# Two attentions over a short context and a self-attention on one core: one list of blocks for all three

## What is computed

```
x  = attention16(x Wq, c Wk, c Wv) + x                     # "a0": 16 heads of 16, 77 keys
n  = layernorm(x);  x = x + Wo attention16(n, n, n)        # "a1": self-attention, 1024 keys
n  = layernorm(x);  x = x + Wco attention16(n, c, c)       # "a2": 77 keys
n  = layernorm(x);  x = x + W2 gelu(W1 n + b1) + b2        # 256 -> 1024 -> 256
```

## Time and profile before

| | |
|---|---|
| median of 3 executions | 869.67 us (863.86, 869.67, 871.61) |
| profiled execution | 873.17 us, its span 871.4 us |
| mean granted TensorE clock | 0.926 of full speed |
| busy: PE, DVE, ACT, POOL | 753.0, 523.6, 424.8, 119.3 us |
| HBM read, written | 36.33 MB, 28.22 MB |

### The profile page before, as it was taken

The page is one execution under the profiler, slowest core; times in us unless marked ns, Lnnn a source line. Parts: engine busy times, 40 slices in busy tenths (PEclk is TensorE's granted clock), DMA queues, the critical chain, the costliest instruction groups (busy, mean ns, idle before and its releaser), DMA issues.

```text
span 871.4 us, 12781 instructions
## 1 busy us (share of the span) xinstructions
PE 753.0 (86%) x4848; PEld 375.3 (43%) x4848; DVE 523.6 (60%) x805; ACT 424.8 (49%) x770; POOL 119.3 (14%) x241
## 2 busy tenths in 40 slices
PE   6428768749899999999999999998978788999998
PEld 3225433334443333333343433333444354457767
DVE  1225465268879999999979998851364456240001
ACT  2105423402068888888767767664534334422120
POOL 9601014021000000000001101020031002130000
PEclk9758878978899999999999999996899899999999
DMA  7765540562580404040404010124154530000001
GB/s 247 209 208 128 111 116 25 185 156 100 197 167 2 76 2 76 3 76 2 75 3 74 3 24 11 44 94 77 41 138 108 137 57 4 1 0 25 19 15 40
DMA packets 37565, 66.95 MB, mean 77 GB/s; under 512 B 6848, under 2 KB 17216, under 8 KB 37504
## 3 DMA queue, kind: packets, MB, share of 16 engines
q1 hardware_dynamic: 37216, 66.05, 30.0%
q10 hardware_dynamic: 288, 0.08, 0.0%
HBM read 36.33 MB, written 28.22 MB: 74 GB/s over the span
## 4 chain that ended last, share of the span: by engine, by line
PE 56%; DVE 21%; SPq 8%; DMA 7%; ACT 3%; issue 3%; POOL 2%; DVEq 0%; POOLq 0%; ACTq 0%
PE PV L727 13%; DVE nm L918 13%; PE ST L711 11%; PE ST L619 5%; PE ST L615 5%; PE SM L656 4%; SPq L476 4%; DMA stacks<-mrow 3%; PE SM L606 3%; PE SM L596 3%; PE SM L600 2%; PE SM L663 2%; POOL stacks L1014 2%; SPq L533 2%; PE PV L619 2%
## 5 line engine op out<-in xcount | busy, mean ns | idle before, releaser
L816 ACT ACTIVATE prob<-ST 128x512 f32<-128x512 f32 (+1 forms) x640 | 344.6, 595 | 215.1 <-PE ST L711 207.0
L918 DVE TENSOR_REDUCE nm<-SM 128x2 f32<-128x1024 f32 x256 | 308.8, 1221 | 18.6 <-PE SM L656 17.0
L727 PE MATMUL PV<-prob,Vst 128*32 128x256 f32 (+1 forms) x2304 | 208.1, 434 | 7.3 <-ACT pvT L805 6.7
L711 PE MATMUL ST<-stacks 64*128 64x512 f32 x512 | 133.9, 506 | 1.5 <-DVE split L852 1.3
L656 PE MATMUL SM<-stacks 64*128 64x512 f32 x512 | 111.3, 430 | 21.2 <-DMA stacks<-k_rows 11.7
L711 PEld LDWEIGHTS ST<-stacks 64*128 64x128 f32 x512 | 51.1, 186 | 111.0 <-ACT prob L816 91.2
L727 PEld LDWEIGHTS PV<-prob,Vst 128*32 128x32 f32 x2304 | 46.6, 110 | 103.6 <-issue 77.4
L921 DVE TENSOR_REDUCE nm<-SM 128x8 f32<-128x624 f32 x64 | 51.5, 805 | 64.1 <-PE SM L663 62.8
L711 PE MATMUL ST<-stacks,Kc 128*77 128x512 f32 x128 | 52.4, 491 | 34.2 <-DMA stacks<-mrow 32.8
L656 PEld LDWEIGHTS SM<-stacks 64*128 64x128 f32 x512 | 49.9, 189 | 44.2 <-DVE nm L918 22.9
L1084 POOL CAST mp<-na 128x16 fp32r<-128x16 f32 x48 | 9.6, 199 | 417.0 <-DVE na L953 253.5
(11 more groups left out here) (98 smaller groups left out, 674.5 us busy)
## 6 DMA issues: line engine op xcount, KB each, us to landing
q_rows<-split SPq DMA_DIRECT2D x72, 256.0 KB
stacks<-q_rows SPq DMA_DIRECT2D x48, 384.0 KB
k_rows<-split SPq DMA_DIRECT2D x24, 256.0 KB
stacks<-k_rows SPq DMA_DIRECT2D x16, 384.0 KB
stacks<-mrow SPq DMA_DIRECT2D x192, 4.0 KB
fm<-in_xT SPq DMA_DIRECT2D x4, 512.0 KB, 8.8
X<-in_x SPq DMA_DIRECT2D x4, 512.0 KB, 4.5
V<-in_w SPq DMA_DIRECT2D x2, 1024.0 KB, 9.5
```

Source lines behind the costliest of these rows:

```text
L711: mm(ST[0:att.keys, n % 3, :], keys_of(att, g, h, kt), QST[att.name][g % att.buffers][rows, h // 2, j * BLK:(j + 1) * BLK], start=True, st ...
L727: last = mm(PV[h * 32:(h + 1) * 32, queries], Vst[:, g % 2, kt, h, :], prob[:, t % 2, h, queries], start=(kt == 0 and first == 0), stop=(k ...
L816: act_fn(prob[0:att.keys, t % 2, h, :], ST[0:att.keys, n % 3, :], ACT.Exp, scale=SCALE) \
L918: ins = vec.tensor_reduce(nm[:, q % 2, c, tile, 2 * n:2 * n + 2], ps.rearrange("p (s k) -> p s k", s=2), AX.X, ALU.max, negate=True)
```

## The change

Blocks of all three attentions now stand in one list, cut into three parts: `FIRST_PART` (a0), `LONG_PART` (a1's 16 blocks, and among the last four of them a2's eight blocks of batch 0, in pairs), `LAST_PART` (a2's eight blocks of batch 1). The blocks are numbered through; maxima, rows, outputs and semaphores count by that number. With it:

- Batch 1's residual adds, norms, transposes, eight chunks and eight value projections move from the list ahead of a1 to steps 1 to 41 of `LONG_PART`. The self-attention output projection and a2's queries of batch 0 stand at steps 67 to 90, one item a step instead of one in two.
- Batch 0's feed-forward (`up` 0 and 1, `down` 0 and 1) moves into `BEFORE_LAST`, ahead of batch 1's a2; `AFTER_LAST` keeps batch 1's.
- a0 and a2 get query buffers of their own, `Qx`, three instead of four, and values of their own, `Vx`. a1 has two stack buffers instead of three, `split` three instead of four. The query projection of a2 and the output projection keep weights of their own.
- Stacks are issued at steps set by hand: a0's group g at step 2g - 4, a1's at 16g - 16, a2's group 7 at step 2 of `LAST_PART`.
- a1's lead is 24 units instead of 26.
- The first memsets (keys' stack, three query stacks, zeros) move from POOL to DVE, ahead of DVE's copy of the context. The DMA that clears the rows of maxima reads 128 columns sixteen times instead of 1024 columns twice. The order of the chunks under a0's last steps is by features first; a1's first stack is issued at step 14 of a0.

```diff
-SB = 4
+SB = 3
...
-A0 = Attention(0, 1, CTX, lead=6, rows_ahead=2, rows_at=0, buffers=4, under=UNDER_A0)
-A1 = Attention(1, SEQ // P, P, lead=26, rows_ahead=1, rows_at=4, buffers=3, under=UNDER_A1)
-A2 = Attention(2, 1, CTX, lead=6, rows_ahead=2, rows_at=0, buffers=4, under=UNDER_A2)
+A0 = Attention(0, 1, CTX, buffers=3)
+A1 = Attention(1, SEQ // P, P, buffers=2)
+A2 = Attention(2, 1, CTX, buffers=3)
...
+class Part:
+
+    def __init__(self, blocks, lead):
+        self.b0, self.t0, self.lead = len(BLOCKS), len(STEPS), lead
+        for att, q in blocks:
+            BLOCK_AT[att.name, q] = len(BLOCKS)
+            FIRST.append(len(STEPS))
+            STEPS.extend((len(BLOCKS), kt) for kt in range(att.kt))
+            BLOCKS.append((att, q))
+        self.steps = len(STEPS) - self.t0
+        self.last = self.steps + 3
+        self.under = {}
+        stream = [("max", b, v) for b in range(self.b0, len(BLOCKS)) for v in range(BLOCKS[b][0].units)]
+        ends, n = {}, 0
+        for b in range(self.b0, len(BLOCKS)):
+            n += BLOCKS[b][0].units
+            ends[b] = n
+        self.before = list(stream[:lead])
+        pending = list(range(self.b0, len(BLOCKS)))
+        added = 0
+        while pending and ends[pending[0]] <= lead - 1:
+            b = pending.pop(0)
+            late = 4 if BLOCKS[b][0].whole else 1
+            self.before.insert(min(ends[b] + late, lead) + added, ("rows", b, 0))
+            added += 1
+        self.work, done = [], lead
+        for i in range(self.last):
+            upto = min(len(stream), lead + 2 * (i + 1))
+            work = [((k + 1) * QUAD // (upto - done) - 1, w) for k, w in enumerate(stream[done:upto])]
+            if pending and ends[pending[0]] <= done:
+                work.append((2, ("rows", pending.pop(0), 0)))
+            done = upto
+            if 2 <= i < self.steps + 2:
+                b, kt = STEPS[self.t0 + i - 2]
+                if kt == BLOCKS[b][0].kt - 1:
+                    work.append((3, ("out", b, 0)))
+            self.work.append(work)
...
+FIRST_PART = Part([(A0, q) for q in range(NQ)], lead=6)
+LONG_PART = Part([(A1, q) for q in range(13)] + [(A2, 0), (A2, 1), (A1, 13), (A2, 2), (A2, 3), (A1, 14), (A2, 4), (A2, 5),
+                                                 (A1, 15), (A2, 6), (A2, 7)], lead=24)
+LAST_PART = Part([(A2, q) for q in range(NQ // 2, NQ)], lead=6)
+for tb in range(NB):
+    FIRST_PART.put(tb, ("load", tb))
+for g in range(3, NG):
+    FIRST_PART.put(2 * g - 4, ("stack", "a0", g))
+FIRST_PART.put(8, ("load", 4), ("load", 5))
+FIRST_PART.put(9, ("x1", 0))
+FIRST_PART.put(10, ("norm", 0, 0), ("x1", 1), ("load", 6), ("load", 7))
+FIRST_PART.put(11, ("norm", 0, 1), *block_of("t_ln1", 0))
+FIRST_PART.put(12, ("proj_q1", 0, 0), ("proj_k1", 0, 0), *block_of("t_ln1", 1))
+FIRST_PART.put(13, ("proj_q1", 1, 0), ("proj_k1", 1, 0))
+FIRST_PART.put(14, ("proj_q1", 0, 1), ("proj_k1", 0, 1), ("stack", "a1", 0))
+FIRST_PART.put(15, ("proj_q1", 1, 1), ("proj_k1", 1, 1))
+LONG = LONG_PART.at
+LONG_PART.put(1, ("x1", 2), ("keys", "a2"))
+LONG_PART.put(4, ("x1", 3))
+LONG_PART.put(5, ("norm", 0, 2))
+LONG_PART.put(7, *block_of("t_ln1", 2))
+LONG_PART.put(8, ("norm", 0, 3))
+LONG_PART.put(10, *block_of("t_ln1", 3))
+LONG_PART.row(11, 2, halves(("proj_q1", "proj_k1"), (2, 3)) + block_of("vals_s", 2) + block_of("vals_s", 3))
+LONG_PART.row(LONG(A1, 8, 3), 1,
+              block_of("t_a1", 0) + block_of("out_1", 0) + [("stats", 1, 0)]
+              + block_of("t_a1", 1) + [("norm", 1, 0)] + block_of("out_1", 1) + [("stats", 1, 1)]
+              + block_of("t_ln2", 0) + [("norm", 1, 1), ("proj_q2", 0, 0)] + block_of("t_ln2", 1)
+              + [("proj_q2", 1, 0), ("proj_q2", 0, 1), ("proj_q2", 1, 1)])
+for g in range(2, NG):
+    LONG_PART.put(max(LONG(A1, 2 * g - 2), 28 if g >= QUAD else 0), ("stack", "a1", g))
+LONG_PART.put(LONG(A1, 11), ("values", "a2", 0), ("stack", "a2", 0))
+LONG_PART.put(LONG(A1, 11, 2), ("stack", "a2", 1))
+LONG_PART.put(LONG(A1, 12), ("stack", "a2", 2))
+LONG_PART.put(LONG(A2, 2), ("stack", "a2", 3))
+LONG_PART.put(LONG(A1, 15, 0), ("ffn", 0))
+LONG_PART.put(LONG(A1, 15, 2), *block_of("t_a1", 2))
+LONG_PART.row(LONG(A1, 15, 3), 1, block_of("out_1", 2))
+LONG_PART.put(LONG(A1, 15, 6), ("stats", 1, 2))
+LONG_PART.put(LONG(A1, 15, 7), ("norm", 1, 2))
+LONG_PART.put(LONG(A2, 7), *block_of("t_ln2", 2))
+BEFORE_FIRST = [("proj_k0", 0), ("proj_q0", 0), ("keys", "a0"), ("proj_q0", 1), ("stack", "a0", 0), ("vals_c", 0),
+                ("values", "a0", 0), ("stack", "a0", 1), ("proj_q0", 2), ("stack", "a0", 2), ("proj_q0", 3),
+                ("side", FIRST_PART, 0, len(FIRST_PART.before))]
+BEFORE_LONG = [("vals_s", 0), ("vals_s", 1), ("values", "a1", 0), ("proj_kc", 0), ("stack", "a1", 1),
+               ("side", LONG_PART, 0, len(LONG_PART.before))]
+BEFORE_LAST = [("t_a1", 3), ("out_1", 3), ("proj_q2", 2), ("norm", 1, 3), ("t_a2", 0), ("out_2", 0), ("t_ln2", 3),
+               ("norm", 2, 0), ("proj_q2", 3), ("stack", "a2", 4), ("t_a2", 1), ("out_2", 1), ("stack", "a2", 5),
+               ("norm", 2, 1), ("t_ln3", 0), ("up", 0), ("t_ln3", 1), ("stack", "a2", 6),
+               ("side", LAST_PART, 0, 3), ("up", 1), ("side", LAST_PART, 3, 6), ("down", 0),
+               ("side", LAST_PART, 6, len(LAST_PART.before)), ("down", 1)]
+LAST_PART.put(2, ("stack", "a2", 7))
+AFTER_LAST = [("t_a2", 2), ("t_a2", 3), ("out_2", 2), ("out_2", 3), ("norm", 2, 2), ("norm", 2, 3),
+              ("t_ln3", 2), ("t_ln3", 3), ("up", 2), ("up", 3), ("down", 2), ("down", 3)]
+PLAN = [(BEFORE_FIRST, FIRST_PART), (BEFORE_LONG, LONG_PART), (BEFORE_LAST, LAST_PART), (AFTER_LAST, None)]
...
+        Qx = sb("Qx", [P, A0.buffers, PAIR, SEQ], F32R)
+        QST = {"a0": [Qx[:, n] for n in range(A0.buffers)], "a1": Qst}
+        QST["a2"] = QST["a0"]
...
             def stack(att, g):
-                n = g % att.buffers
-                if g >= att.buffers:
-                    sp.wait_ge(st_done, (att.t0 + (g - att.buffers + 1) * HALVES * att.kt) * QUAD)
-                elif (att.name, g) in AFTER_GROUP:
-                    old, last = AFTER_GROUP[att.name, g]
-                    sp.wait_ge(st_done, (old.t0 + (last + 1) * HALVES * old.kt) * QUAD)
+                k = att.nth + g
+                n = k % att.buffers
+                if k >= att.buffers:
+                    sp.wait_ge(st_done, QUAD * (end_of(A1, (g - A1.buffers) * HALVES + HALVES - 1) if att.whole
+                                                else cross_end(k - att.buffers)))
-                if g == 0 or att is A2 and g == 2:
+                if k == 0:
+                    sp.wait_ge(stacks_padded if att.whole else pad_ready, 1)
...
+            vec.memset(Kc[:, :, :, :, :].bitcast(FP32), 0.0).then_inc(keys_zero, 1)
+            dve.wait_ge(keys_zero, 1)
+            for s in range(2):
+                vec.memset(Kc[s * HALF + 32:(s + 1) * HALF, :, :, s, :].bitcast(FP32), 1.0)
+            for tile in QST["a0"]:
+                pad(tile, 0.0)
+            vec.memset(zeros[:, :], 0.0).then_inc(pad_ready, 1)
             dve.wait_ge(in_k0, 16 * 3)
             vec.tensor_copy(ctxT[:, :, :, CTX:CTXP], ctxT[:, :, :, CTX - 1:CTX]).then_inc(ctx_padded, 1)
...
-            for tile in QST["a0"]:
-                pad(tile, 0.0)
-            padded()
+            step(gp.memset(Vx[:, :, :, :, :], 0.0))
+            step(gp.memset(Vx[0:CTX, :, :, :, HD:HD + 1], 1.0))
+            step(gp.memset(prob[64:P, :, :, :], 0.0))
+            step(gp.memset(nexp[:, :], -0.5))
+            step(space())
+            pool.wait_ge(pad_ready, 1)
+            space().then_inc(pad_ready, 1)
+            step(space())
             step(gp.memset(Vst[:, :, :, :, :], 0.0))
             step(gp.memset(Vst[:, :, :, :, HD:HD + 1], 1.0))
-            step(gp.memset(prob[64:P, :, :, :], 0.0))
-            step(gp.memset(mp[:, :, :].bitcast(FP32), 0.0))
-            step(gp.memset(nexp[:, :], -0.5))
-            padded()
-            pad(Kst[1], 1.0)
-            pad(Kst[2], 1.0)
+            for n in range(A1.buffers):
+                pad(Kst[n], 1.0)
+                pad(Qst[n], 0.0)
+            space().then_inc(stacks_padded, 1)
```

562 lines of the change are left out of this document (236 added, 326 removed).

## The result

The changed kernel takes **948.12 us** (median of 4, 940.62 to 953.42) where the kernel before takes 869.09 beside it (863.86 to 871.61): ratio 1.091, 95% interval 1.081 to 1.101. The forecast was 917, in a range of 882 to 945. The sign was right; the size was not: +79 us, where the sum said +47. The profiled execution has a span of 950.4 (before 871.4) and a mean granted clock of 0.901 (before 0.926).

What follows compares the result with a forecast made beforehand. It took PE and VectorE to be full in the self-attention and PE in the feed-forward, so only PE's idle time elsewhere could be won. Terms summed to +47 us: 920.2 from the profiled 873.2, 917 against the median; range 882 to 945.

Steps and rivals of the forecast that it cites:

- the term of the first attention's queries: First attention: with three buffers, stacks issued one step ahead land late, PE waits 7.7 us in groups 3 to 7; +30.
- Group 7's wait in step 11: First attention, step 11, which waits for norms today: PE's wait for the last query stack adds 2 us.
- the memsets: Start: memsets moved to VectorE delay its context copy and everything after it; +11, bounds +2 and +16.
- the moved work: Self-attention: batch 1's chunks, value projections, transposes, adds and norms cost time under its full steps; +44, bounds 22 and 52.
- The bridge: Stretch from first attention to self-attention: batch 1's work leaves, stack wait, maxima and a row transpose stay; -29, bounds -24, -36.
- The split buffers: First attention's four steps with two chunks each: three buffers shrink PE's run-ahead over SyncE's stores; +3, bounds 0 and +7.
- The two stack buffers: Self-attention: stacks issued four steps ahead fall about 0.3 us short where no item lengthens the steps; +1, bounds 0 and +6.
- The waits at the self-attention's end: Self-attention's end: a 3.7 us wait for last-attention queries and 9 us of low clock leave; -13, bounds -6 and -15.
- The other order of last attention and feed-forward: After and under the self-attention: waits that leave offset new ones, including group 7's 9.2 us; 0, bounds -12 and +15.
- the queries land in time: Rival, first and last attention: stacks land within 2 us of the need, so query waits fall away; 878 us, chance 0.10.
- the self-attention takes the work in: Rival, self-attention: moved work and batch 0's attention steps fit into PE's and VectorE's mutual waits; 843 us, chance 0.09.
- The rival of a clock that stays down: Rival, after six query waits: low clock persists, steps at half speed add about 5 us each; 945 us, chance 0.10.

Runs made afterwards that it cites:

- late stacks alone: Kernel before, with only the first attention's query stacks 3 to 7 issued behind step 2g-4 instead of 2g-6, still four buffers: 912.3 us, ratio 1.049.
- the run with all gains together: Changed kernel with four query buffers in first and last attention, batch 1's work back ahead of the self-attention, memsets on POOL: 865.4 us, ratio 0.998.
- group 7 mended: Changed kernel with four query buffers in first and last attention, so the last one's group 7 stack goes out with group 6's: 897.2 us, ratio 1.032.
- the run with the work back in the bridge: Changed kernel with batch 1's adds, norms, transposes, projection chunks and value projections back ahead of the self-attention: 929.3 us, ratio 1.070.
- items in every step: Kernel before, with the first batch's 24 items one in every self-attention step from step 67, instead of every second step: 869.5 us, ratio 1.000.

## Why the forecast was right in sign and wrong in size

**The step that failed is the term of the first attention's queries, +30.** Its mechanism was right: late stacks alone, put into the old kernel, cost 43 us, and taking them back out of the new one gives back 38 with 6 us of its start lost by my edit. Its size was not. The stack's landing was taken as 6.0 us after its first issue, from the end of the DMA activity in the earlier trace rows; to the second wait's end it is 7.6 us in the old kernel with late stacks and 7.9 to 8.6 in the new one and its variants with the same plan, because the release comes 1.5 to 2 us after the bulk of the traffic. The short pieces of the zeros have no part that a run shows. For the first wait, whose stack goes out behind an input load, and the fourth it is up to 9.8. The slow steps behind a wait cost 2.4 us and not 1.5. Over steps 0 to 9 that is 90.5 us in the changed kernel's trace against 77.2 forecast, four waits being 42.1 against 33.4 and the work between them 48.4 against 43.8. Three other traces of these steps have 85.8 to 87.2, so some 4 of the 13 us are that execution's. Group 7's wait in step 11 adds 5 and not 2.

**Right in size:** the memsets (+11; 13 by medians, 9 at the first score), the moved work (+44; +46.6).

**The bridge** (-29; -31.4) came out with its sizes off against each other. Its stack's first issue and PE's first maximum are these rows:

```profile
228.11 0.70 SPq L512 DMA_DIRECT2D stacks<-zeros  x1
242.21 0.73 PE L671 MATMUL SM<-stacks 64*128 64x512 f32 x4
```

The stack went out 3.7 us ahead of the last values and not 2 behind them (228.11 against 231.81), and PE's first maximum came 10.4 us behind them, without a wait for the stack, and not 15; the maxima and the rows took 2 us more than forecast.

**The split buffers** (+3) cost 5 us in steps 12 to 15, in the changed kernel and by themselves; by medians of the whole run it is 1.7, with an interval that reaches 5.

**The two stack buffers** (+1) cost some 1.6 us in the changed kernel (its seventh block is 22.9 us), and so little only because the moved work hid them: without it the first five blocks are 8 us longer than bare ones (4.5 in the run with all gains together). The forecast's condition, "where no item lengthens them", was the right one.

**The waits at the self-attention's end** (-13) are worth 6.5 by medians. The term took its low clock from one execution for a forecast of a median, and that execution was one of the two with the long low clock.

**The other order of last attention and feed-forward** (0) came to +7 by the stages: 211.9 - 235.3 = -23.4, and 30 of that are the steps moved away. Group 7's wait with its low clock was 11, the difference between 208 and 197 us behind the self-attention; the forecast had named it at 9.2 and set it against gains. With group 7 mended the same count gives 197 - 235 + 30 = -8, a gain and not 0. The 30 is an estimate (eight steps at 3.78), so how much of the 8 is this order's is not shown. The forecast gap of 4 to 5 us before the last `up` is there, 3.5 and 2.2 us before the last transposes.

**The four blocks with batch 0's items**, 7.7 us longer than the same items elsewhere, had no term at all. Some 2.3 of it is low clock; the cause of the other 5 stays open.

**The rivals.** That the queries land in time and that the self-attention takes the work in are both out, by the run with late stacks and the run with the work back in the bridge. The rival of a clock that stays down named 945 and comes nearest to the time; but it wanted 5 us more at each of six waits, and 1 was found (2.4 against 1.5). Most of the excess is the wait itself. It was near for another reason.

The Trainium skill, "DMA: Bandwidth & Descriptors", section "Anatomy of one DMA — SWDGE (gpsimd) path", gives 2.0 us plus the bytes at 436 GB/s for a DMA on GpSimd's path. The stacks are issued by SyncE, so the figure is for another path; as an estimate it would give 3.8 us for a stack's two halves of 393 KB. The trace has 7.9 (112.50 to 120.37), and the measurement decides.

## What to carry to other kernels

Price a wait for a transfer from its issue to the first instruction that it releases, on a row where some engine really waits for it, not to the end of DMA activity. A buffer fewer turns "issued three steps ahead" into "one step ahead" long before any engine looks busier; look first for memory that is idle in that stretch, as half of a later stack was here. A wait on the engine that issues all DMAs is never alone: ask which semaphores a moved issue stands behind, and what is queued behind it.

## What the runs showed of the hardware

- Behind a wait of 3.0 to 3.7 us at the self-attention's end, the clock was at 0.50 for some 21 us in the kernel before and for 18 with items in every step, but for 8 us with three split buffers and 9 with late stacks. The first and the third differ by 6 us in the time of two blocks. A term for the clock that is taken from one trace carries that much doubt.
- From the first issue of a query stack (two DMAs of 384 KB and two small ones) to the start of a PE that waits for it, the traces have 7.5 to 10.7 us, 1.5 to 2 of it behind the bulk of the traffic in the one read closely.
- A memset on VectorE of 32 x 2048 elements took 1.76 us, 0.86 ns a column, with 0.46 us between two of them, so 1.09 ns with the gap:

```profile
6.72 1.76 DVE L1002 MEMSET Qx<- 32x2048 f32 x1 [0.46 <-issue]
8.95 1.76 DVE L1002 MEMSET Qx<- 32x2048 f32 x1 [0.46 <-issue]
```

The Trainium skill, "VectorE: DVE Perf Modes", section on zero memsets issued as uint32, has one cycle per element, 1.04 ns at the 0.96 GHz of its first table; the instruction itself was quicker, and the measurement decides. With the gaps the total (the copy at 19.78) was as forecast.
